# Attention maxima: the causal mask moved from TensorE's matmuls into VectorE's maximum

## The chip, the cores and the metric

One core of a Trainium2 chip runs the whole program in one launch. The metric is the device time in microseconds (us). All data are in float32 unless a line says otherwise; the scores of the attention are made from bf16 parts, three for each number, so that they come out close to float32.

## What is computed

Two hybrid layers act on a residual x of 4 sequences of 1024 tokens with 256 channels: a Mamba block, a feed-forward block, causal attention, the feed-forward block again, then a linear attention, a mixture of experts, a second linear attention with a GELU block, and the mixture of experts again. The change is in the causal attention (16 heads of 16 channels), of which the reference is, cut to what matters:

```python
q, k, v = (split(q), split(k), split(v))
q = apply_rope(q, sin, cos)
k = apply_rope(k, sin, cos)
scores = jnp.einsum('bhqd,bhkd->bhqk', q, k) / jnp.sqrt(jnp.float32(dh))
causal = jnp.triu(jnp.ones((T, T), dtype=bool), k=1)
scores = jnp.where(causal[None, None], jnp.float32(-1000000000.0), scores)
attn = jax.nn.softmax(scores, axis=-1)
out = jnp.einsum('bhqk,bhkd->bhqd', attn, v)
```

## The kernel before

The stages run one after another with a barrier between them. `stage_attn` takes the sequences one by one in a loop of four passes. A pass has two parts: a preparation (norm, projection, rotary embedding, bf16 parts of q and k, their transposes), and `heads(b)`, the attention itself.

In `heads` the 16 heads are taken in four quarters (`QUADS`) of four heads (`HG`, index `j`). The scores are computed twice. First with queries on the partitions (`scores_q`, L1117 to L1128), only for the row maxima: VectorE takes the maximum of every piece in `chunk_max` (L1398). Then with keys on the partitions (`scores_k`, L1130 to L1144), where two extra rows of q and k bring in minus the row's maximum, and ScalarE takes the exponential (`exps`, L1311). `values` (L1156) then multiplies the exponentials by v on TensorE.

A quarter has 12 steps (`PER`), numbered 0 to 11 here. Step by step and for each of its four heads, a piece of `scores_q` has 128, 256, 384, 512, 512, 128, 512, 256, 512, 384, 512 and 512 columns (`CHUNKS`), and a piece of `scores_k` has 512, 384, 256, 128, 512, 512, 512, 512, 512, 384, 256 and 128 (`STEPS`). Of the pieces of `scores_q` those of the steps 0, 1, 2, 3, 5, 7, 9 and 11 end on the diagonal. There a second matmul, identity times the table `causal` (0 and -1e9, bf16), adds the mask onto the last 128 columns (L1126). `scores_k` does the same on its side (L1142); that is not touched.

The order of the work is written out by hand. TensorE runs `scores_q` one whole quarter (`LEAD` = 12 steps) ahead of `scores_k`. So a pass of `heads` begins with 12 steps of `scores_q` alone (called the lead here), goes on with three quarters in which, head by head, `scores_k` and `scores_q` alternate and `values` of the step before closes each step, and ends with one quarter without `scores_q` (the tail). The PSUM banks 0 to 2 are a ring for the pieces of `scores_q`: TensorE waits in `slot` until VectorE has counted `ring_used` for the piece three items back. Banks 3 to 5 are the same for `scores_k`, freed by the exponentials.

Twice a quarter, after step 3 and after step 11, VectorE runs `block_max` (L1410, L1413, L1415: the maximum of a half, its sign turned, and two bf16 parts). TensorE transposes the result in `max_transpose` (L1165) in the following step (step 4 or step 0), behind the `scores_q` of head 1, and waits for it in its order; VectorE copies it out (L1422). In the steps 2 and 6 TensorE also runs `turn` (L1173), whose result VectorE normalises (L1429, L1431).

Of the kernel before, what the change touches and what calls it, by code (L numbers as in the profile page):

```python
# [18 lines left out]
AX = mybir.AxisListType  # L19

P = 128
# [3 lines left out]
GT = 4  # L25
# [941 lines left out]
KS = PARTS * AD  # L967
# [12 lines left out]
SLOTS = 3  # L980
# [4 lines left out]
def stage_attn(c):  # L985
    nc = c.nc
    with Local(c, "attn") as s:
        banks = s.ps("banks", [P, 8, 512])
# [4 lines left out]
        causal = s.sb("causal", [P, 3, P], BF16)  # L993
# [19 lines left out]
        ov = ra[:, :, :, :].rearrange("p a h d -> p (a h d)")  # L1013
        rec = s.sb("rec", [P, 2, GT, HG])
# [5 lines left out]
                 "m_loaded st_filled exp_ready pv_done vh_ready ov_ready rec_ready oT_filled oT_ready y_ready y_used consts zeroed parts_seen")  # L1020
        S = {n: s.sem(n) for n in names.split()}

        def sem(n):
            return S[n]
# [40 lines left out]
        with nc.Block() as block:  # L1065
# [18 lines left out]
            def _(pe):  # L1084
# [32 lines left out]
                def scores_q(b, m, j):  # L1117

                    at_ring = slot(b, ("chunk", m, j))
                    h = m // PER * HG + j  # L1120
                    qt, at, size = CHUNKS[m % PER]
                    diag = at + size == (qt + 1) * P
                    mm = pe.matmul(banks[:, at_ring, 0:size], qT[0:KS, qt // GT, h, qt % GT * P:(qt % GT + 1) * P],  # L1123
                                   kT[0:KS, h, at:at + size], start=True, stop=not diag, skip_group_check=True)
                    if diag:
                        mm = pe.matmul(banks[:, at_ring, size - P:size], causal[:, 2, :], causal[:, 0, :],  # L1126
                                       start=False, stop=True, skip_group_check=True)
                    mm.then_inc(sem("ring_filled"), 1)  # L1128
# [229 lines left out]
            def _(dve):  # L1358
# [39 lines left out]
                def chunk_max(b, m, j):  # L1398

                    qt, at, size = CHUNKS[m % PER]  # L1400
                    item = AT["chunk", m, j]
                    dve.wait_ge(sem("ring_filled"), b * RING + item + 1)
                    dve.tensor_reduce(mp[:, qt // GT, j, qt % GT, at // 512:at // 512 + 1], banks[:, item % SLOTS, 0:size], AX.X,  # L1403
                                      ALU.max).then_inc(sem("ring_used"), 1)
# [51 lines left out]
                dve.memset(mp[:, :, :, :, :], -3e38).then_inc(sem("consts"), 1)  # L1456
                dve.wait_ge(sem("loaded"), 16 * 10)
                dve.wait_ge(sem("lora_filled"), 1)
# [1581 lines left out]
```

## Time and profile before

| | us |
|---|---|
| median of 3 runs | 4031.93 (4028.64 to 4040.47) |
| the profiled execution's own time | 4033.2 |
| its span in the trace | 4031.1 |
| TensorE busy (PE) | 3271.0, 81% of the span |
| VectorE busy (DVE) | 2663.5, 66% |
| ScalarE busy (ACT) | 1691.3, 42% |
| matmul L1123, `scores_q` | 274.3, 768 pieces |
| VectorE L1403, the maxima | 382.2, 768 pieces |

The shares are means over eight different stages. The attention's four passes lie between about 1459 and 2366 us and repeat every 228.6 us; a reader has to look at the windows within one pass. A matmul's busy time is partly the time that its result is under way, so the distance between the starts of two matmuls, not their duration, is what one costs.

### The profile page before, as it was taken

Reading aid. Unit: us, or ns where it says so; the run is one execution under the profiler, and the core shown is the slowest. Engines: PE = TensorE matmul, PEld = TensorE weight load, DVE = VectorE, ACT = ScalarE, POOL = GpSimd, SP = SyncE. Lnnn points to the kernel's source line nnn. Section 1 sums busy time; section 2 is a strip of 40 time slices with the busy share of each in tenths; the row PEclk is TensorE's granted clock in tenths of the full one; section 3 lists DMA queues with packets and bytes.
Section 4 is the critical chain, followed back from the end, with each engine's and each line's share of the span. In section 5 each row is a group of like instructions: output and inputs, shape, how many; then the busy total and the mean of one; then the engine's idle time right before and its main releaser. Section 6 shows DMA issues by size and latency. Waiting matters only on the chain. (4 is left out here: it accounts for less than half of the span.)

```text
span 4031.1 us, 55646 instructions
## 1 busy us (share of the span) xinstructions
PE 3271.0 (81%) x16440; PEld 1865.4 (46%) x16441; DVE 2663.5 (66%) x5097; ACT 1691.3 (42%) x3279; POOL 1379.0 (34%) x1379
## 2 busy tenths in 40 slices
PE   4877787788658969889897989876886788898885
PEld 1333333333225654444444446554465467566464
DVE  2998899899967757575765757597434766223435
ACT  3655545555515535556464655311222223222221
POOL 2777777677730020110202000143454200001453
PEclk9988898899889988979798999988898889999998
DMA  2544545454520000000000000350134578000146
GB/s 89 137 124 118 122 125 126 115 132 129 132 75 1 0 15 2 2 2 2 1 2 2 2 1 0 98 145 0 50 121 138 138 143 96 18 16 0 61 127 199
DMA packets 370275, 283.15 MB, mean 70 GB/s; under 512 B 214026, under 2 KB 290366, under 8 KB 370016
## 3 DMA queue, kind: packets, MB, share of 16 engines
q1 hardware_dynamic: 356960, 246.43, 24.7%
q0 software_dynamic: 13056, 33.65, 2.5%
q8 instruction: 117, 1.92, 0.2%
q14 instruction: 142, 1.16, 0.1%
HBM read 205.69 MB, written 76.16 MB: 70 GB/s over the span
## 5 line engine op out<-in xcount | busy, mean ns | idle before, releaser
L428 POOL TENSOR_TENSOR mamba_dBu<-mamba_du,mamba_bcs 128x512 f32<-128x512 f32 x512 | 642.0, 1269 | 272.1 <-DMA mamba_bcs<-mamba_bc 206.5
L378 PE MATMUL mamba_banks<-mamba_hc,ident 128*128 128x512 f32 x1024 | 557.0, 667 | 214.7 <-DVE mamba_hc L598 152.7
L551 ACT ACTIVATE mamba_banks<-mamba_delta,mamba_a_neg 128x512 f32<-128x512 f32 x512 | 352.1, 691 | 241.2 <-DVE mamba_hc L598 232.2
L1403 DVE TENSOR_REDUCE attn_mp<-attn_banks 128x1 f32<-128x512 f32 (+3 forms) x768 | 382.2, 551 | 96.5 <-PE attn_banks L1126 53.8
L378 PEld LDWEIGHTS mamba_banks<-mamba_hc,ident 128*128 128x128 f32 x1024 | 195.3, 209 | 538.3 <-DVE mamba_hc L598 308.6
L591 DVE TENSOR_TENSOR_SCAN mamba_banks<-mamba_banks,mamba_dBu 128x512 f32<-128x512 f32 x256 | 312.3, 1220 | 92.0 <-POOL mamba_dBu L428 58.0
L598 DVE TENSOR_TENSOR mamba_hc<-mamba_banks,mamba_bcs 128x512 f32<-128x512 f32 x512 | 346.1, 677 | 21.2 <-PE mamba_banks L378 21.1
L591 DVE TENSOR_TENSOR_SCAN mamba_banks<-mamba_banks,mamba_h_end,mamba_dBu 128x512 f32<-128x512 f32 x256 | 329.0, 1286 | 28.7 <-ACT mamba_banks L551 20.6
L1123 PE MATMUL attn_banks<-attn_kT,attn_qT 96*128 96x512 bf16 (+3 forms) x768 | 274.3, 374 | 10.0 <-ACT attn_kT L1292 5.0
L1311 ACT ACTIVATE attn_probs<-attn_banks 128x512 f32<-128x512 f32 (+1 forms) x384 | 182.1, 528 | 180.3 <-PE attn_banks L1142 155.8
L1139 PE MATMUL attn_banks<-attn_qT,attn_kT 98*128 98x512 bf16 (+3 forms) x768 | 248.6, 339 | 10.2 <-ACT attn_probs L1311 5.3
L823 PE MATMUL ffn_hp<-ffn_xT,ffn_w1T 128*128 128x512 f32 x512 | 230.3, 605 | 11.0 <-ACT ffn_xT L160 7.5
L1311 ACT ACTIVATE attn_r<-attn_banks 128x128 f32<-128x128 f32 (+2 forms) x384 | 155.1, 459 | 84.3 <-PE attn_banks L1142 52.6
L1881 POOL DMA_INDIRECT moe_rows<-moe_yb,moe_xg x144 | 141.7, 984 | 137.0 <-issue 73.1
L835 PE MATMUL ffn_yp<-ffn_w2T,ffn_hs 128*128 128x256 bf16 x1536 | 170.0, 273 | 0.0
L835 PEld LDWEIGHTS ffn_yp<-ffn_w2T,ffn_hs 128*128 128x128 bf16 x1536 | 150.3, 98 | 18.4 <-issue 0.7
L823 PEld LDWEIGHTS ffn_hp<-ffn_xT,ffn_w1T 128*128 128x128 f32 x512 | 96.7, 193 | 134.0 <-issue 111.8
L322 PE MATMUL mamba_banks<-mamba_xT,mamba_win 128*128 128x512 f32 x256 | 131.6, 643 | 28.6 <-ACT mamba_sz L504 27.4
L2225 DVE TENSOR_TENSOR moe_h<-moe_hp,moe_silu 128x128 f32<-128x128 f32 x144 | 42.0, 292 | 170.2 <-ACT moe_silu L2070 170.2
L1270 POOL COPY attn_vh<-attn_v 128x512 f32<-128x512 f32 x16 | 13.2, 842 | 408.3 <-PE attn_banks L1156 408.3
L1974 PE MATMUL moe_hp<-moe_we,moe_xgT 128*128 x576 | 152.7, 388 | 0.0
L1139 PEld LDWEIGHTS attn_banks<-attn_qT,attn_kT 98*128 98x128 bf16 x768 | 75.3, 99 | 155.7 <-ACT attn_r L1311 68.7
(374 smaller groups left out, 6584.2 us busy)
## 6 DMA issues: line engine op xcount, KB each, us to landing
mamba_bcs<-mamba_bc SPq DMA_DIRECT2D x256, 512.0 KB, 4.9
moe_slots_moe<-moe_pad SPq DMA_DIRECT2D x2, 9252.0 KB, 52.3
moe_xg<-moe_slots_moe SPq DMA_DIRECT2D x144, 128.5 KB, 2.1
mix_qkv<-mixA_qkv SPq DMA_DIRECT2D x8, 1536.0 KB, 6.0
mixA_y<-moe_rows SPq DMA_DIRECT2D x16, 512.0 KB, 5.7
mix_qk<-mix_qkv SPq DMA_DIRECT2D x16, 512.0 KB, 7.4
mix_v<-mix_qkv SPq DMA_DIRECT2D x16, 256.0 KB, 7.5
mix_out<-mixB_oh SPq DMA_DIRECT2D x16, 256.0 KB, 7.3
```

The lines of the kernel that those rows point to most:

```text
L378: pe.matmul(banks[:, SUMS + k % PAIR, :], c.ident[:, :], hc[:, n % RING, :], start=(st == 0), stop=True, skip_group_check=True).then_inc(s ...
L428: pool.tensor_tensor(dBu[:, n % RING, :], du[:, v, k, :], bcs[:, i_of(n) % 4, 0, :], ALU.mult)\
L551: act.activation(banks[:, n % RING, :], delta[:, v, k, :], ACT.Exp, scale=a_neg[:, k, st:st + 1])\
L591: dve.tensor_tensor_scan(banks[:, n % RING, :], banks[:, n % RING, :], dBu[:, n % RING, :], 0.0 if v == 0 else h_end[:, st, k:k + 1], ALU. ...
L598: dve.tensor_tensor(hc[:, n % RING, :], banks[:, n % RING, :], bcs[:, (p * NS + st) % 4, 1, :], ALU.mult).then_inc(sem("hc_ready"), 1)
L823: mm = pe.matmul(hp[:, b % 4, :], w1T[:, k, b * P:(b + 1) * P], norm.xT[:, k, :], start=(k == 0), stop=(k == KD - 1))
L835: mm = pe.matmul(yp[:, j, :], hs[:, v, b, a, j * P:(j + 1) * P], w2T[:, b, :], start=(b == 0 and a == 0), stop=(b == HB - 1 and a == SP_ - 1))
L1123: mm = pe.matmul(banks[:, at_ring, 0:size], qT[0:KS, qt // GT, h, qt % GT * P:(qt % GT + 1) * P], kT[0:KS, h, at:at + size], start=True, s ...
L1139: mm = pe.matmul(banks[:, bank, 0:size], kT[:, h, kt * P:(kt + 1) * P], qT[:, n % 2, h, at - n % 2 * 512:at - n % 2 * 512 + size], start=T ...
L1311: act.activation(probs[step % 2][:, j, 0:size], banks[:, SLOTS + (step * HG + j) % SLOTS, 0:size], ACT.Exp, scale=AD ** -0.5)\
L1403: dve.tensor_reduce(mp[:, qt // GT, j, qt % GT, at // 512:at // 512 + 1], banks[:, item % SLOTS, 0:size], AX.X, ALU.max).then_inc(sem("rin ...
L1974: mm = pe.matmul(gup[r % 2], xgT[:, r % 2, k * P:(k + 1) * P], we[:, :, :].rearrange("p e n -> p (e n)")[:, bass.ds(at + k * 2 * P, 2 * P) ...
```

## The change

`scores_q` no longer issues the mask matmul; it is one matmul for every piece. A new float32 table `later` of 128 by 512 holds zeros in its first 384 columns and the triangle of the mask in the last 128. In `chunk_max`, a piece that ends on the diagonal is no longer reduced by `tensor_reduce`. VectorE reads the piece from PSUM and the last columns of `later` from SBUF, adds them, writes the sum back to PSUM, and gives the maximum, all by `tensor_tensor_reduce`. In front of it stands a count of a new semaphore, `diag_seen`, which takes the wait for the matmul. The other pieces stay as they are. The table is filled once at the stage's start.

```diff
+        later = s.sb("later", [P, 512])
...
-                    diag = at + size == (qt + 1) * P
-                    mm = pe.matmul(banks[:, at_ring, 0:size], qT[0:KS, qt // GT, h, qt % GT * P:(qt % GT + 1) * P],
-                                   kT[0:KS, h, at:at + size], start=True, stop=not diag, skip_group_check=True)
-                    if diag:
-                        mm = pe.matmul(banks[:, at_ring, size - P:size], causal[:, 2, :], causal[:, 0, :],
-                                       start=False, stop=True, skip_group_check=True)
-                    mm.then_inc(sem("ring_filled"), 1)
+                    pe.matmul(banks[:, at_ring, 0:size], qT[0:KS, qt // GT, h, qt % GT * P:(qt % GT + 1) * P],
+                              kT[0:KS, h, at:at + size], start=True, stop=True).then_inc(sem("ring_filled"), 1)
...
+                    to = mp[:, qt // GT, j, qt % GT, at // 512:at // 512 + 1]
                     dve.wait_ge(sem("ring_filled"), b * RING + item + 1)
-                    dve.tensor_reduce(mp[:, qt // GT, j, qt % GT, at // 512:at // 512 + 1], banks[:, item % SLOTS, 0:size], AX.X,
-                                      ALU.max).then_inc(sem("ring_used"), 1)
+                    if at + size == (qt + 1) * P:
+                        dve.sem_inc(sem("diag_seen"), 1)
+                        dve.tensor_tensor_reduce(banks[:, item % SLOTS, 0:size], banks[:, item % SLOTS, 0:size], later[:, 512 - size:512], 1.0, -3e38,
+                                                 ALU.add, ALU.max, to).then_inc(sem("ring_used"), 1)
+                    else:
+                        dve.tensor_reduce(to, banks[:, item % SLOTS, 0:size], AX.X, ALU.max).then_inc(sem("ring_used"), 1)
...
                 dve.memset(mp[:, :, :, :, :], -3e38).then_inc(sem("consts"), 1)
+                dve.memset(later[:, 0:512 - P], 0.0)
                 dve.wait_ge(sem("loaded"), 16 * 10)
+                dve.tensor_copy(later[:, 512 - P:512], causal32[:, 0, :]).then_inc(sem("causal_at_end"), 1)
+                dve.wait_ge(sem("causal_at_end"), 1)
                 dve.wait_ge(sem("lora_filled"), 1)
```

## Rows read from the trace of the kernel before

**Rows 1.** Windows of pass one: length, busy PE, PEld, DVE, ACT, POOL, PEclk, DMA, GB/s.
```profile
1514.00:1537.40 23.40, 21.14 (x81) 6.88 (x82) 22.40 (x50) 0.00 (x0) 0.00 (x0) 0.57 0.01 1
1537.40:1572.80 35.40, 34.56 (x257) 16.03 (x256) 26.49 (x60) 22.27 (x49) 0.00 (x0) 0.90 0.01 2
1572.80:1606.50 33.70, 32.52 (x270) 15.02 (x266) 26.37 (x61) 22.21 (x50) 0.62 (x1) 1.00 0.01 2
1606.50:1640.20 33.70, 32.52 (x270) 15.02 (x266) 26.36 (x61) 22.21 (x50) 0.61 (x1) 1.00 0.01 2
1640.20:1667.00 26.80, 23.41 (x180) 8.17 (x177) 3.02 (x10) 20.21 (x49) 0.00 (x0) 1.00 0.01 2
```

**Rows 2.** Timeline of VectorE in the lead: start, length, instruction, count, idle before.
```profile
1514.55 6.90 DVE L1403 TENSOR_REDUCE attn_mp<-attn_banks 128x1 f32<-128x128 f32 x16 [3.54 <-PE attn_banks L1126]
...
1523.35 15.37 DVE L1403 TENSOR_REDUCE attn_mp<-attn_banks 128x1 f32<-128x512 f32 x30
```

**Rows 3.** Waits in the lead: who waited for whom, us in total, times, longest.
```profile
PEld attn_banks L1123 <- DVE attn_mp L1403: 14.4, 38, 0.7
```

**Rows 4.** Timeline of TensorE in step 9 of the third quarter, one head and `values`.
```profile
1633.15 0.33 PE L1139 MATMUL attn_banks<-attn_qT,attn_kT 98*128 98x384 bf16 x1
1633.32 0.22 PE L1142 MATMUL attn_banks<-attn_causal 128*128 128x128 bf16 x1
1633.37 0.33 PE L1123 MATMUL attn_banks<-attn_kT,attn_qT 96*128 96x384 bf16 x1
1633.54 0.22 PE L1126 MATMUL attn_banks<-attn_causal 128*128 128x128 bf16 x1
1633.60 0.33 PE L1139 MATMUL attn_banks<-attn_qT,attn_kT 98*128 98x384 bf16 x1
...
1634.58 1.07 PE L1156 MATMUL attn_banks<-attn_probs,attn_vh 128*32 128x512 f32 x8
```

**Rows 5.** Timeline around step 3 and step 4 of the third quarter, VectorE's rows.
```profile
1615.98 2.47 DVE L1403 TENSOR_REDUCE attn_mp<-attn_banks 128x1 f32<-128x512 f32 x4
1618.49 0.19 DVE L1410 TENSOR_REDUCE attn_nm<-attn_mp 128x16 f32<-128x32 f32 x1
...
1620.22 0.20 DVE L1422 COPY attn_nmT<-attn_banks 32x128 bf16<-32x128 bf16 x1
1620.35 1.86 DVE L1403 TENSOR_REDUCE attn_mp<-attn_banks 128x1 f32<-128x512 f32 x4
```

**Rows 6.** The same stretch, TensorE's transpose of the maxima.
```profile
1619.24 0.22 PE L1165 MATMUL attn_banks<-attn_causal,attn_nmb 128*32 128x128 bf16 x1 [0.53 <-DVE attn_nmb L1415]
```

**Rows 7.** Steps 10 and 11 of the third quarter: VectorE's eight maxima, then TensorE's transpose.
```profile
1636.17 4.94 DVE L1403 TENSOR_REDUCE attn_mp<-attn_banks 128x1 f32<-128x512 f32 x8 [0.87 <-PE attn_banks L1123]
...
1641.90 0.22 PE L1165 MATMUL attn_banks<-attn_causal,attn_nmb 128*32 128x128 bf16 x1 [0.85 <-DVE attn_nmb L1415]
```

**Rows 8.** Timeline of TensorE in step 5 of the third quarter, first and fourth head.
```profile
1621.04 0.39 PE L1139 MATMUL attn_banks<-attn_qT,attn_kT 98*128 98x512 bf16 x1
...
1622.20 0.39 PE L1139 MATMUL attn_banks<-attn_qT,attn_kT 98*128 98x512 bf16 x1
```

**Rows 9.** Groups of VectorE's instructions by shape: busy us, mean ns, idle before.
```profile
L598 DVE TENSOR_TENSOR mamba_hc<-mamba_banks,mamba_bcs 128x512 f32<-128x512 f32 x512 | 346.1, 677 | 21.2 <-PE mamba_banks L378 21.1
L591 DVE TENSOR_TENSOR_SCAN mamba_banks<-mamba_banks,mamba_dBu 128x512 f32<-128x512 f32 x256 | 312.3, 1220 | 92.0 <-POOL mamba_dBu L428 58.0 <-ACT mamba_banks L551 32.6 <-issue 0.2
L1403 DVE TENSOR_REDUCE attn_mp<-attn_banks 128x1 f32<-128x512 f32 x384 | 238.7, 682 | 41.3 <-PE attn_banks L1123 38.7 <-PE attn_banks L1126 2.0
```

**Rows 10.** Timeline: four small instructions of VectorE in a row, in the norm.
```profile
1684.44 0.38 DVE L120 BATCH_NORM_AGGREGATE attn_moments<-attn_bn_stats 128x2 f32<-128x6 f32 x4
```

**Rows 11.** Window of the first quarter's start.
```profile
1537.40:1544.50 7.10, 6.79 (x39) 4.15 (x41) 4.44 (x15) 4.28 (x8) 0.00 (x0) 0.50 0.01 1
```

**Rows 12.** Timeline of the stage's start.
```profile
1441.21 0.51 ACT L1334 CAST attn_causal<-attn_ra 128x384 bf16<-128x384 f32 x1 [26.97 <-DMA attn_ra<-in_causal_dram]
...
1445.13 1.42 DVE L1461 SCALAR_TENSOR_TENSOR attn_w<-attn_banks,attn_w 128x256 f32<-128x256 f32 x4 [7.89 <-PE attn_banks L1198]
```

More of the change, by code:

```diff
@@ L1019, in stage_attn @@
                  "stT_filled evac_act evac_dve ring_filled ring_used max_ready part_ready m_ready "
-                 "m_loaded st_filled exp_ready pv_done vh_ready ov_ready rec_ready oT_filled oT_ready y_ready y_used consts zeroed parts_seen")
+                 "m_loaded st_filled exp_ready pv_done vh_ready ov_ready rec_ready oT_filled oT_ready y_ready y_used consts zeroed parts_seen diag_seen causal_at_end")
         S = {n: s.sem(n) for n in names.split()}
```

## The prediction

> **What bounds the kernel now.** The page's chain of work that ended last stays inside the last mixture-of-experts stage and says nothing of the attention. So I read the windows of one pass of `heads` first, and then the timelines of its engines.
>
> The windows [rows 1] show three different parts. In the lead, 23.4 us, VectorE is busy for 22.4 us; TensorE's weight loads for `scores_q` wait 14.4 us for L1403 [rows 3]. The lead is VectorE's. Its 48 maxima, with the first `block_max` between them, run from 1514.55 to 1538.72 us [rows 2], that is 24.2 us. In the second and third quarter, 33.7 us each, TensorE is busy for 32.5 us and VectorE for 26.4 us: these are TensorE's on the whole. The tail, 26.8 us, has no `scores_q` and stays as it is.
>
> Inside a TensorE-bound quarter there are two stretches that VectorE sets nevertheless. After step 3 TensorE reaches the transpose of the maxima and stands for 0.53 us until VectorE's `block_max` is done [rows 6]. VectorE had come to step 3's four pieces at 1615.98 us, right from its normalisation, and went through them without a pause to `block_max` at 1618.49 us [rows 5]. After step 11 the same: eight maxima in a row from 1636.17 us, and then TensorE's stop of 0.85 us [rows 7]. What is added to a maximum there arrives whole at TensorE, and what is taken from TensorE there only makes its stop longer.
>
> **Part 1, the matmuls that go.** A mask matmul costs the distance to the next start, not its 0.22 us: L1126 starts at 1633.54 and the next `scores_k` at 1633.60 us, 0.06 us, and the like one at L1142 takes 0.05 to 0.06 us [rows 4]. I take 0.058 us. 32 of them go per quarter, 1.86 us, but not all of it is gained:
> - Steps 3 and 11: nothing, by the two stretches above.
> - Step 0: the transpose stands behind head 1, so the two matmuls before it only lengthen the stop. Two count.
> - Steps 5 and 7: beside 512-column pieces of `scores_k` TensorE is held by the other ring. In step 5 the fourth head starts 1.16 us after the first [rows 8], though three pairs at (512 + 128 + 128)/2.4 columns per ns make 0.96 us; three matmuls less only lengthen that wait, and the fourth, behind it, counts. In step 7 the pieces are 128 columns longer and the fourth head comes just at 1.16 us, so the limit is reached as soon as something goes. One counts in each.
> - Steps 1, 2 and 9: all four each. In step 9 a head takes TensorE 0.45 us and `values` 1 us more per step, 2.8 us together [rows 4]; VectorE has four pieces shorter than those of 512 columns, under 2.4 us. In the steps 1 and 2 the pieces are no longer.
>
> That is 2 + 8 + 1 + 1 + 4 = 16 matmuls, 0.93 us per quarter, 2.8 us per pass. The first quarter's opening 7.1 us run at a granted clock of 0.50 [rows 11], the 1.2 GHz level, where a matmul costs twice as much: six of the counted ones lie there, 0.3 us more. Together 3.1 us per pass.
>
> **Part 2, the maxima that grow.** The pieces of 512 columns are 0.60 us apart: (2.47 - 0.68) / 3 from the four in a row [rows 5, 9]. An addition with one input in PSUM and one in SBUF takes 677 ns for 512 columns where the maximum takes 682 ns [rows 9], so I cost the adding itself at nothing. The unknown is e, what the second result (the maximum beside the written sum) and the extra count cost. No row of this kernel has an instruction with two results. If the maximum is handed out by a small instruction of its own, the nearest rows are the small ones: four of them in a row end within 0.38 us at 0.16 us each, so 0.07 us apart [rows 10], and the 128-column copy of `block_max`'s result holds the next maximum back by 0.13 us [rows 5], of which half is its columns. That gives e = 0.066 us. If that instruction has to wait until the sum is written out, the distance becomes what `block_max` shows behind the last maximum: it starts at 1618.49 where a plain maximum would have been due at 1615.98 + 4 x 0.60 = 1618.38, and 0.07 us of its own come on top, so 0.11 + 0.07 = 0.18 us. Below, e can be zero if both results leave with one instruction; a gain is excluded, since every column is still read once. I take 0.066 us, and for the 8 pieces of 128 columns in a quarter 0.12 us: the first fifteen pieces of the lead, 307 columns on average, are 0.41 us apart, (6.90 - 0.68) / 15 [rows 2], about 1 ns a column, which leaves some 0.2 us for 128 columns, and there the separate count, its arithmetic and two instructions may no longer hide behind the columns. The mean is 0.08 us.
>
> The Trainium skill bears on both questions. VectorE: DVE Perf Modes, section "Two Vector instructions with no wait between them", says that an operation which also gives out its accumulator is two instructions, the main one and a read of the accumulator. No row here shows it; it would make the case of e = 0 wrong. DVE: opcode table, instruction layouts, handler registers and perf-mode slots says under "Feedback" that a stage reading its own last result loses no cycle, while the scan runs at half rate; the scan's 1220 ns against 677 ns [rows 9] agree with its second half, and by its first the running maximum keeps the full rate.
>
> In the lead all 32 grown maxima lie on VectorE's path: 32 x 0.08 = 2.56 us, less some 0.3 us in the first pieces, where at the 1.2 GHz level TensorE is as slow as VectorE. That is 2.3 us per pass. In the three quarters the four maxima of step 3 and the four of step 11 lie on the path: 8 x 0.066 = 0.53 us, 1.6 us per pass. The other 24 lie beside TensorE's work; their cover is 33.7 - 26.4 = 7.3 us per quarter [rows 1], and they take 1.9 us of it.
>
> **Part 3, waits and the rest.** The count of `diag_seen` waits for the matmul in place of the maximum. Behind it on VectorE stand the piece itself and all later ones; for them TensorE's ring and, after steps 3 and 11, its transpose wait. Where VectorE is behind (the lead, steps 3 and 11) the wait is over before it is reached. Where VectorE waits for TensorE, the start comes some 0.1 us later, and the three banks cover it. The table is filled while VectorE waits anyway: ScalarE gets the mask at 1441.21 us, and VectorE's first work after that is at 1445.13 us [rows 12]. A fill of 384 columns and a copy of 128 are under 1 us. Cost nothing; if that cover were gone, 1 us once.
>
> **The sum.** Per pass + 2.3 + 1.6 - 3.1 = + 0.8 us; four passes, + 3 us. From the profiled execution's 4033.2 us (the span 4031.1 and 2.1 around it) that makes 4036 us. That execution lies 1.3 us above the median, so against the median it is 4035.
>
> **The rivals.** In terms of e, a pass changes by 32 e - 0.3 + 24 e - 3.1 us.
>
> A, the read waits. With e = 0.18 us the lead grows by 5.5 and the quarters by 4.3 us, 6.7 us net per pass: 4033.2 + 27 = 4060 us, slower. It decides from e = 0.12 us on, where the four passes lose 12 us. For it: behind the last maximum `block_max` does start late. Against it: that one waits by a semaphore, and small instructions without one follow closely.
>
> B, one instruction. With e near zero only TensorE's gain is left: 3.1 to 3.4 us per pass, 4033.2 - 13 = 4020 us, at the edge of faster. For it: the busy share of TensorE. Against it: a second result to another memory.
>
> C, half rate. If the running maximum costs a second cycle per column like the scan, a 512-column piece takes 1.2 us, and the mean piece of 320 columns grows by 0.40 us. The lead grows by 12.8 us, and VectorE with 26.4 + 12.8 us becomes the bound of the quarters, 5 us above 33.7: 28 us per pass, 4145 us. Against it: nothing goes back to an earlier point as in the scan.
> The Trainium skill's Vector Engine (DVE) Microarchitecture Reference, section "Points that are easy to get wrong", states a halved rate when both sources of such an instruction lie in SBUF and are not bf16. Here one lies in PSUM; if the rule held all the same, the time would be that of C.
>
> D, the clock. The clock rises to 2.4 GHz some 7 us into the first quarter, after TensorE has been without a long stop [rows 1, 11]. A lead with a less busy TensorE can move that. The first quarter is 1.7 us longer than the others for its 7 us at the low level, so 3.4 us more of it cost 0.8 us per pass, 3 us in all, either way. This widens the range and decides nothing.
>
> That the mask is not removed cannot be: the matmul is gone from the code.
>
> **How the numbers follow.** A difference under 0.3%, 12 us, is about what a measurement of this kernel can't tell from no change. My forecast, e between 0.02 and 0.11 us, 4024 to 4044 us, gets 0.52. A gets 0.26, B 0.14, C 0.04, and 0.04 is for what I have not thought of. Of B about two thirds fall below 4020 us, and of the forecast a little, as my count of gained matmuls may be too small: faster 0.13, slower 0.33, within 0.3% 0.54. The range is to leave out no more than 2 in 10: C, the unknown, and the far ends of A and B, so 4018 to 4064 us.
>
> **What would show it.** In the changed profile: no row of L1126, and yet the second and third quarter shorter by 0.4 us (0.93 less 0.53), not by 1.86 us; the lead grows by 2 to 3 us; the rows of VectorE show the new instruction at about 0.68 us for 512 columns and how far the next piece lies behind it; the stop before the transpose is longer than 0.53 and 0.85 us. A distance of 0.67 us between 512-column pieces would prove e right, 0.78 rival A, 0.60 rival B, 1.2 rival C. The working is wrong if the quarters shorten by over 1 us, which would mean that I was wrong on steps 3, 5, 7 and 11.

## The result and the profile after

| | before | after |
|---|---|---|
| median, us | 4030.91 (4025.62 to 4040.47) | 4040.39 (4032.95 to 4045.51) |
| span of the profiled execution, us | 4031.1 | 4034.1 |
| one pass of `heads`, us | 152.8 | 154.3 |
| preparation between two passes, us | 75.8 | 77.8 |
| attention stage, first matmul to the next stage's first, us | 932.0 | 943.5 |

The ratio is 1.0021, 95% interval 1.0015 to 1.0027: 6 to 11 us more (9.5 by the medians). That is inside the forecast's own range of 4024 to 4044 us and within 0.3%, but three times the 3 us that the sum gave. The two spans are only 3.0 us apart, and that agreement with the sum is chance: in these two executions the attention stage differs by 11.5 us, while stages that nobody touched came out shorter (the linear attention 226.6 and 222.3 us, the two mixture-of-experts stages 291.7 and 288.6, 314.0 and 310.9). So the stage is what must be compared. In this trace its 11.5 us are 5.6 us in the four `heads` and 5.9 us in the three preparations between them.

The first pass of the changed kernel in the windows view answers to [rows 1]: window and length, then busy us (and instructions) of PE, PEld, DVE, ACT and POOL, the granted clock, the DMA share and GB/s. The rows are lead, three quarters, tail and preparation.
```profile
1515.80:1540.70 24.90, 21.96 (x50) 5.16 (x51) 23.97 (x79) 0.00 (x0) 0.00 (x0) 0.50 0.01 1
1540.70:1575.70 35.00, 32.86 (x223) 13.72 (x221) 28.26 (x93) 21.90 (x49) 0.00 (x0) 0.90 0.01 2
1575.70:1609.70 34.00, 31.63 (x239) 13.27 (x236) 28.12 (x93) 21.98 (x50) 0.61 (x1) 1.00 0.01 2
1609.70:1643.30 33.60, 31.33 (x238) 13.24 (x234) 27.99 (x93) 21.88 (x50) 0.61 (x1) 1.00 0.01 2
1643.30:1670.10 26.80, 23.25 (x179) 8.09 (x175) 3.15 (x12) 20.12 (x48) 0.00 (x0) 1.00 0.01 2
1670.10:1748.00 77.90, 59.36 (x407) 44.08 (x407) 44.11 (x116) 37.35 (x52) 26.64 (x38) 0.85 0.01 2
```
The lead grew by 1.5 us. The quarters hold 32 matmuls fewer each, with TensorE busy for 31.3 to 31.6 instead of 32.5 us, and yet are as long as before (35.0, 34.0 and 33.6 against 35.4, 33.7 and 33.7). The last row is the preparation, in which no instruction was changed; the same stretch of the kernel before is this:
```profile
1666.90:1742.70 75.80, 56.72 (x407) 41.81 (x407) 43.40 (x116) 37.28 (x52) 26.55 (x38) 0.89 0.01 2
```
The count of matmuls is the same, and VectorE, ScalarE and GpSimd are busy for nearly the same time. TensorE is busy for 2.6 us longer, and its clock is 0.85 instead of 0.89. The granted clock has two levels here, 0.50 (1.2 GHz) and 1.00 (2.4 GHz), so a mean of c means a share of 2 x (1 - c) at the lower one: 0.22 x 75.8 = 17 us before and 0.30 x 77.9 = 23 us after (17.3 and 23.1 us from the stretches themselves).

The grown maxima, grouped by shape, answer to [rows 9]: busy us, mean ns of one, idle before.
```profile
L1402 DVE CUSTOM_DVE_ANT_0 attn_banks<-attn_banks,attn_later 128x512 f32<-128x512 f32 x128 | 84.6, 724 | 1.8 <-PE attn_banks L1123 1.0
L1402 DVE DVE_READ_ACCUMULATOR2_ANT attn_mp<- 128x1 f32 x512 | 72.2, 141 | 0.6
L1402 DVE CUSTOM_DVE_ANT_0 attn_banks<-attn_banks,attn_later 128x128 f32<-128x128 f32 x128 | 37.7, 301 | 22.8 <-PE attn_banks L1123 19.5 <-PE attn_banks L1161 1.3
L1405 DVE TENSOR_REDUCE attn_mp<-attn_banks 128x1 f32<-128x512 f32 x256 | 160.1, 682 | 26.7 <-PE attn_banks L1123 26.7
```
The one call became two instructions, an addition and a read of the accumulator, which the Trainium skill's section "Two Vector instructions with no wait between them" (VectorE: DVE Perf Modes) said; this trace agrees, 512 of each. What they cost shows in the timeline (start, duration, instruction). After step 3, where [rows 5] had four maxima in 2.51 us:
```profile
1618.98 0.69 DVE L1402 CUSTOM_DVE_ANT_0 attn_banks<-attn_banks,attn_later 128x512 f32<-128x512 f32 x1
1619.59 0.14 DVE L1402 DVE_READ_ACCUMULATOR2_ANT attn_mp<- 128x1 f32 x1
1619.59 0.73 DVE L1402 CUSTOM_DVE_ANT_0 attn_banks<-attn_banks,attn_later 128x512 f32<-128x512 f32 x1
1620.23 0.14 DVE L1402 DVE_READ_ACCUMULATOR2_ANT attn_mp<- 128x1 f32 x1
1620.23 0.73 DVE L1402 CUSTOM_DVE_ANT_0 attn_banks<-attn_banks,attn_later 128x512 f32<-128x512 f32 x1
...
1621.53 0.14 DVE L1402 DVE_READ_ACCUMULATOR2_ANT attn_mp<- 128x1 f32 x1
1621.71 0.19 DVE L1411 TENSOR_REDUCE attn_nm<-attn_mp 128x16 f32<-128x32 f32 x1
```
The read starts together with the next addition, so it is hidden for the most part; only at the end of a run of pieces does it stand alone. The pieces start 0.65 us apart where plain maxima start 0.60 apart: e is 0.05 us, for 512, 384 (0.515 against 0.465) and 256 columns (0.382 against 0.331). For 128 columns, in the first step of the lead, they are 0.31 to 0.34 us apart, against 0.199 for plain maxima that TensorE doesn't hold up, so e is 0.12 us. (In the kernel before those pieces lay 0.214 us apart, because TensorE had two matmuls for each at 1.2 GHz.) The four pieces and the start of `block_max` take 1621.71 - 1618.98 = 2.73 us, 0.22 more than before.

TensorE's stops before the transpose of the maxima, answering to [rows 6] and [rows 7]:
```profile
1622.46 0.21 PE L1161 MATMUL attn_banks<-attn_causal,attn_nmb 128*32 128x128 bf16 x1 [0.74 <-DVE attn_nmb L1416]
...
1645.12 0.22 PE L1161 MATMUL attn_banks<-attn_causal,attn_nmb 128*32 128x128 bf16 x1 [1.06 <-DVE attn_nmb L1416]
```
They were 0.53 and 0.85 us. Both are 0.21 us longer.

### The profile page after: what moved, and what is told of

It reads as the page before. It is cut to its first block and busy times, and to the rows that moved or that the text cites. A ratio compares the mean times of both kernels' runs of the same rounds, so it can differ in the third digit from the quotient of the medians.

```text
span 4034.1 us, 55648 instructions
## 1 busy us (share of the span) xinstructions
PE 3263.4 (81%) x15928; PEld 1843.1 (46%) x15929; DVE 2691.8 (67%) x5611; ACT 1687.1 (42%) x3279; POOL 1383.6 (34%) x1379
## 3 DMA queue, kind: packets, MB, share of 16 engines
q1 hardware_dynamic: 356960, 246.43, 24.7%
## 5 line engine op out<-in xcount | busy, mean ns | idle before, releaser
L378 PE MATMUL mamba_banks<-mamba_hc,ident 128*128 128x512 f32 x1024 | 557.8, 667 | 217.2 <-DVE mamba_hc L598 154.3
L598 DVE TENSOR_TENSOR mamba_hc<-mamba_banks,mamba_bcs 128x512 f32<-128x512 f32 x512 | 344.3, 674 | 19.8 <-PE mamba_banks L378 19.5
L1123 PE MATMUL attn_banks<-attn_kT,attn_qT 96*128 96x512 bf16 (+3 forms) x768 | 278.7, 378 | 19.5 <-DVE attn_mp L1402 6.8
L1402 DVE CUSTOM_DVE_ANT_0 attn_banks<-attn_banks,attn_later 128x384 f32<-128x384 f32 (+3 forms) x512 | 240.5, 517 | 49.8 <-PE attn_banks L1123 43.7
L1885 POOL DMA_INDIRECT moe_rows<-moe_yb,moe_xg x144 | 141.7, 984 | 133.8 <-issue 73.3
L1405 DVE TENSOR_REDUCE attn_mp<-attn_banks 128x1 f32<-128x512 f32 x256 | 160.1, 682 | 26.7 <-PE attn_banks L1123 26.7
```

Of the source, the lines that this page charges most:

```text
L378: pe.matmul(banks[:, SUMS + k % PAIR, :], c.ident[:, :], hc[:, n % RING, :], start=(st == 0), stop=True, skip_group_check=True).then_inc(s ...
L598: dve.tensor_tensor(hc[:, n % RING, :], banks[:, n % RING, :], bcs[:, (p * NS + st) % 4, 1, :], ALU.mult).then_inc(sem("hc_ready"), 1)
L1402: dve.tensor_tensor_reduce(banks[:, item % SLOTS, 0:size], banks[:, item % SLOTS, 0:size], later[:, 512 - size:512], 1.0, -3e38, ALU.add, ...
```

## The experiments

### Gain and cost apart

The first three kernels each do one part of the change. Gain alone: one matmul per piece and the plain maximum, so the maxima are taken of unmasked scores.
```diff
-                    if diag:
-                        mm = pe.matmul(banks[:, at_ring, size - P:size], causal[:, 2, :], causal[:, 0, :],
-                                       start=False, stop=True, skip_group_check=True)
```


> The kernel before without the mask matmuls of scores_q, and with the plain maximum for every piece: part 1 of the sum alone. Left out is the mask for the maxima: a row's maximum takes in the later keys of its diagonal block; the exponentials are masked as before. By my sum only 16 of the 32 matmuls of a quarter are gained: lead unchanged at 23.4 us, second and third quarter 33.7 - 0.93 = 32.8 us, stops before the transpose longer, 3.1 us per pass and 12 us in all, ratio 0.997. If all 32 counted, a quarter would fall by 1.9 us and the ratio would be 0.994. If the repeating pattern of clock stretches settles on another one, a pass can move by 2 us more or less than that, outside heads.

Measured: ratio 0.9980, 95% interval 0.9970 to 0.9989, 7 to 8 us less. `heads` took 148.8 to 150.3 us, 149.7 in the mean. Its second pass in the windows view (lead, first and second quarter of the three that overlap):
```profile
1746.60:1769.50 22.90, 20.72 (x49) 5.08 (x50) 22.23 (x50) 0.00 (x0) 0.00 (x0) 0.50 0.01 1
1769.50:1804.60 35.10, 33.73 (x224) 13.83 (x222) 26.30 (x60) 22.03 (x49) 0.00 (x0) 0.87 0.01 1
1804.60:1837.40 32.80, 31.16 (x238) 13.23 (x234) 26.13 (x61) 21.89 (x50) 0.62 (x1) 1.00 0.01 2
```
The second quarter lost 1.0 us where 0.93 was forecast, and the lead 0.5 us where nothing was. `heads` lost 3.1 us a pass, as forecast, but partly by luck: the first quarter lost 0.8 us in the mean (33.7 to 35.1 us, against 35.3) where 1.2 was forecast. The attention stage fell by less than the four `heads` (8.8 against 12.5 us), because its first preparation, ahead of pass one, took 76.0 instead of 72.9 us in this trace, with 36.3 instead of 31.9 us at 1.2 GHz.

Cost alone: the changed kernel with its mask matmuls kept, so that the mask is added twice.
```diff
+                    if diag:
+                        mm = pe.matmul(banks[:, at_ring, size - P:size], causal[:, 2, :], causal[:, 0, :],
+                                       start=False, stop=True, skip_group_check=True)
```


> The changed kernel with the mask matmuls put back: VectorE adds the table and takes the maximum, TensorE's work is that of before (the mask is added twice): part 2 alone. The changed kernel's trace has the pieces 0.05 us further apart (0.12 us for those of 128 columns). If these simply lie on VectorE's path in the lead and after steps 3 and 11, the lead grows by 32 x 0.067 = 2.1 us, and each quarter by 8 x 0.05 = 0.4 us: 3.4 us per pass, 13.5 us in all, ratio 1.0034. If the clock's pattern takes part, the part of a pass outside heads changes too, by up to 2 us per pass, though no instruction there differs: ratio up to 1.005.

Measured: ratio 1.0049 (1.0036 to 1.0063), 20 us more (22 by the medians). `heads` took 156.7 to 158.2 us, 157.2 in the mean. Its first pass:
```profile
1519.90:1545.20 25.30, 23.27 (x81) 6.20 (x82) 24.19 (x81) 0.00 (x0) 0.00 (x0) 0.53 0.01 1
1545.20:1581.20 36.00, 34.65 (x257) 15.81 (x256) 28.36 (x93) 22.23 (x49) 0.00 (x0) 0.91 0.01 2
1581.20:1615.90 34.70, 32.96 (x271) 14.85 (x268) 28.14 (x93) 22.31 (x50) 0.61 (x1) 1.00 0.01 2
```
The lead grew by 2.0 us (forecast 2.3), each quarter by 0.7 to 0.95 (forecast 0.53). In `heads` the parts add up: against the mean of 152.8 us, 4.4 - 3.1 = + 1.3 us a pass, and the changed kernel has + 1.4 in the mean of its four passes. The cost is larger than forecast in the quarters and smaller in the lead.

Count alone: the kernel before, with only the extra count ahead of each diagonal piece, which takes the wait for the matmul.
```diff
+                    if at + size == (qt + 1) * P:
+                        dve.sem_inc(sem("diag_seen"), 1)
                     dve.tensor_reduce(mp[:, qt // GT, j, qt % GT, at // 512:at // 512 + 1], banks[:, item % SLOTS, 0:size], AX.X,
```


> The kernel before with the extra count of diag_seen ahead of the plain maximum of each piece on the diagonal, and nothing else: the wait is taken by a separate instruction. If the added cost of a piece is the read of the maximum alone, the pieces of 512 columns stay 0.60 us apart and those of 128 columns 0.20 us, and the time is that of before (ratio 1.000). If the separate wait is what makes 128 columns cost 0.12 us more, their distance rises toward 0.3 us, the lead grows by up to 0.8 us, and maxima that wait for TensorE start about 0.13 us later: ratio up to 1.002.

Measured: ratio 1.0030 (1.0019 to 1.0042), 12 us more. That is no less than the whole change costs, and it is not where the count is. The lead took 24.0 instead of 23.4 us, the second quarter 33.9 instead of 33.8. Pieces of 128 columns stay 0.22 to 0.24 us apart in the first step of the lead, so the count by itself does not make the 0.12 us; maxima that wait for TensorE do start 0.11 us later. The sum of the four `heads` even fell, from 611.3 to 608.3 us, because the first quarter of the second, third and fourth pass ran almost wholly at 2.4 GHz. The three preparations rose from 227.5 to 241.3 us. The first quarter of its second pass, and the preparation ahead of that pass:
```profile
1667.00:1747.40 80.40, 61.67 (x407) 45.14 (x408) 44.20 (x116) 37.36 (x52) 26.82 (x38) 0.83 0.01 2
...
1771.30:1804.60 33.30, 32.30 (x257) 14.56 (x255) 26.45 (x60) 21.72 (x49) 0.00 (x0) 0.98 0.01 2
```
The preparation has the same 407 matmuls, but TensorE is busy in it for 61.7 instead of 56.7 us at a clock of 0.83. With an edit of some 0.1 us at some of VectorE's instructions, stretches at 1.2 GHz left the first quarter (1.2 instead of 7.1 us of it) and lay in the preparation (27.3 instead of 17.3 us). One trace shows where they lay; the 12 us of the seven timed runs agree with its stage, 944.0 against 932.0 us.

### A version that masks on the engine that has time

If the step-by-step account is right, the mask belongs to TensorE where VectorE sets the pace (the lead, the steps 3 and 11), and to VectorE everywhere else.
```diff
+        def by_matmul(m):
+            return m < PER or m % PER in (GT - 1, PER - 1)
...
-                    diag = at + size == (qt + 1) * P
+                    diag = at + size == (qt + 1) * P and by_matmul(m)
...
+                    if at + size == (qt + 1) * P and not by_matmul(m):
```


> The changed kernel with the mask matmul and the plain maximum kept in the lead and in the steps 3 and 11, and the added table everywhere else (steps 0, 1, 2, 5, 7 and 9 of the three quarters that overlap with scores_k). If the lead and these two steps are where the longer maxima hurt, nothing is lost any more and TensorE's gain stays: by my sum 0.93 us per quarter, about 3 us per pass, ratio 0.997. If the three banks of the ring do not cover the longer and later maxima, about half of it is left, ratio 0.9985. If the loss lies elsewhere, the ratio is 1.002 as for the whole change.

Measured: ratio 0.9967 (0.9956 to 0.9977), 13 us less than before (16 by the medians), with the full mask. The lead is again 23.4 us, the second and third quarter 33.1 us each, against 33.7 before. `heads` took 150.9, 149.0, 149.9 and 150.9 us. The preparations were unequal among themselves, 76.7, 79.4 and 73.3 us. The last of them:
```profile
2124.20:2197.50 73.30, 53.87 (x407) 40.08 (x408) 43.96 (x116) 37.21 (x52) 26.21 (x38) 0.93 0.01 2
```
Again 407 matmuls, now in 53.9 busy us at a clock of 0.93. The attention stage is 9.0 us shorter than before, 923.0 against 932.0 us. The traced execution as a whole is not (span 4031.0 us, as before; its time lies 17 us above this kernel's median): its Mamba stage took 1151.8 instead of 1147.4 us and other untouched stages were longer too.

### Moving the lead without changing it

The next question was whether a mere shift in time, with no change at TensorE or the maxima, moves the clock. In the kernel before, VectorE fills a scratch tile once, twice or four times before the first maximum of each pass.
```diff
+                    for i in range(4):
+                        dve.memset(pad[:, :], 0.0).then_inc(sem("padded"), 1)
+                        dve.wait_ge(sem("padded"), b * 4 + i + 1)
```


> The kernel before with one fill of an unused tile of 768 columns on VectorE at the start of heads, about 0.8 us, and its wait. Nothing else is changed, neither TensorE's work nor the maxima. If a pass is just the sum of its parts, it grows by 0.8 us and the whole by 3 us, ratio 1.0008. If the repeating pattern of clock stretches matters, a pass can stay at 228.6 us or jump toward 232 us, the difference lying in parts where no instruction changed.

> The same with two fills, 1.6 us, as much as the changed kernel's heads grew by. Plain sum: 1.6 us per pass, 6.5 us in all, ratio 1.0016, and the preparation between two heads as long as before (75.8 us from the last scores_k to the next scores_q). Clock pattern: a pass of 232 us as in the changed kernel, with 77.9 us of preparation, ratio 1.003.

> The same with four fills, 3.2 us. Plain sum: 3.2 us per pass, 13 us in all, ratio 1.0032. Clock pattern: the pass is again 232 us, since it is already that long with half the delay, or jumps once more, to 235 us and more; the preparation then makes up the difference to the sum, in either direction.

Measured, on one chip: 0.9984 (0.9975 to 0.9993), 0.9979 (0.9971 to 0.9988) and 1.0004 (0.9995 to 1.0012). As delays they failed. Four fills, in VectorE's timeline:
```profile
1508.81 0.70 DVE L1439 MEMSET attn_pad<- 128x768 f32 x1 [0.23 <-DVE attn_pad L1439]
1509.64 2.54 DVE L1404 TENSOR_REDUCE attn_mp<-attn_banks 128x1 f32<-128x128 f32 x8
```
VectorE has 3.5 us to wait for TensorE's first piece in any case [rows 2], and four fills only just use that up. The lead stayed at 23.4 to 23.8 us, `heads` at about 153 (but for the first pass of the version with two fills, 150.7 us), the preparations between passes at 75.2 to 76.0, the stage at 931.6, 932.8 and 932.5 us. In that one pass the first quarter had 1.6 us at 1.2 GHz instead of 7, and the preparation ahead of it took 75.9 instead of 72.9 us: a shift like that of the count alone, smaller. The medians differ for all that, by up to 10 us, while in the traces the attention stage is the same to 1.2 us. What differs there lies in the linear attention and the mixture of experts behind it (222.2 and 288.8, 222.1 and 287.7, 226.8 and 291.6 us; before 226.6 and 291.7). The Mamba stage can't be called an effect of the fills: it took 1144.8, 1144.6 and 1142.3 us, and in two traces of the kernel before 1147.4 and 1143.2. So a difference of 0.2% is measurable here and can still say nothing of the edited code. The question itself stays open, since nothing was shifted.

### Both kernels again

> The kernel before once more, unchanged: how far two series of the same program lie apart (ratio 1.000 within 0.001), and whether its profile shows the same clock pattern: 17.3 us at the 1.2 GHz level and 75.8 us of preparation between two heads, 228.6 us per pass. If the pattern differs from execution to execution, one profile of each kernel cannot show what the change did to it.

> The changed kernel once more, unchanged, beside the kernel before on the same chip: ratio 1.002. If its clock pattern belongs to the program, the preparation is 77.8 us again with 23.4 us at the low level. If it is drawn anew each time, the preparation is anything between 73 and 80 us; heads stays at 154.2 us, give or take 1 us for its own low stretch.

Measured: the kernel before against itself 1.0005 (0.9996 to 1.0014), the changed one 1.0023 (1.0013 to 1.0033), as the first time. The stage took 932.7 and 942.1 us. In the changed kernel `heads` again took 154.5 us (153.8 to 155.1), 5.9 us more in the four passes than the kernel before. The preparations between the passes this time were 75.8, 76.8 and 75.7 us, 1.1 more, and the one ahead of the first pass 76.1 against 73.2 us, 2.9 more (in the first pair of traces the two were alike, 73.2 and 72.9). The first of them, changed kernel:
```profile
1672.00:1747.70 75.70, 56.65 (x406) 41.70 (x406) 43.41 (x116) 37.20 (x52) 26.60 (x38) 0.89 0.01 2
```
So the cost in `heads` belongs to the kernel, while the 6 us in the three preparations of the first trace don't come in every execution of it. The unchanged kernel before differs too: 16.5 to 16.6 of the lead's 23.4 us lay at 1.2 GHz in three passes of this trace, 20.0 in all passes of its first trace, and the lead was as long in both.

### Is it the lead's idle TensorE?

One theory was that the lead with fewer matmuls leaves TensorE less busy, and that this keeps the clock low for longer. This kernel is the changed one with the mask matmuls back in the lead alone (where the mask is then added twice).
```diff
-                    diag = at + size == (qt + 1) * P
+                    diag = at + size == (qt + 1) * P and m < PER
```


> The changed kernel with the mask matmuls put back in the lead only, where VectorE is the bound and TensorE has time for them (the mask is added twice there). If the missing activity of TensorE in the lead is what lengthens the low stretch around the start of the first quarter (31.2 us of a heads at the low level against 27.0 us before), it goes back to 27 us and the first quarter loses about 0.5 to 1 us, ratio 1.001. If the low stretch is set by the times at which the parts of a pass fall, nothing changes systematically, and the ratio stays at 1.002.

Measured: ratio 1.0046 (1.0032 to 1.0059), 8 to 9 us above the changed kernel. `heads` is the same, 154.3 to 154.7 us, and 30.7 to 31.6 us of it at the low level did not go back to 27. The preparations took 80.7, 77.8 and 80.5 us, 10.7 us more than the changed kernel had on that chip, which is the whole difference of the stages but 0.5 us (953.3 against 942.1). The first one:
```profile
1674.80:1755.50 80.70, 62.03 (x406) 45.42 (x406) 44.24 (x116) 37.35 (x52) 26.79 (x38) 0.83 0.01 2
```
The theory falls: with more matmuls in the lead the time at 1.2 GHz grew, in this preparation to 27.3 us from 23.1 and 17.3 in the two traces of the changed kernel.

### Gain alone and the selective version again

> The kernel without mask matmuls and without the added table once more (left out is the mask for the maxima alone; the exponentials are masked). Its heads was 150.0 us where the kernel before has 152.8; so four passes give 11 us, ratio 0.9972, if the rest of the program lies as before. It had 0.998 the first time. If it is the better of the two versions, it is not above the selective one here.

> The selective kernel once more. Its heads was 149.0 to 150.9 us, that of the kernel without any mask for the maxima 148.8 to 150.3, so the two should be alike, ratio 0.997 to 0.998; the first time it had 0.9967. Its preparations were 73.3 to 79.4 us with 10.4 to 23.9 us at the low level: if that belongs to the program, a spread of this size comes again, if not, they are 75.8 us.

Measured on another chip, where the kernel before has a median of 4117.14 us: 0.9976 (0.9967 to 0.9986) and 0.9974 (0.9960 to 0.9988). The ratios hold. The 85 us by which everything is longer there lie mostly in the two mixture-of-experts stages (329.6 and 353.9 us in the selective version's trace, 292.4 and 313.2 before); the attention stage took 922.4 and 923.5 us, as on the first chip. Gain alone had `heads` of 149.8, 150.3, 150.0 and 149.7 us and preparations of 77.9, 75.7 and 75.7: as on the first chip, but for the first pass and the preparation behind it (148.8 and 76.8 there). Of the selective version `heads` (151.1, 149.0, 149.9 and 150.9 us) and the preparations (76.7, 79.4 and 73.3 us, with 19.5, 23.9 and 10.3 us at 1.2 GHz) came out as on the first chip to 0.2 us. The pattern of the preparations is thus no accident of one execution of this version. That of the changed kernel did not come again, as shown above.

## Why the prediction was right or wrong, point by point

All kernels in one table, us, lead and second quarter from the first pass, the preparations those between the passes:

| kernel | lead | second quarter | mean `heads` | preparations | stage |
|---|---|---|---|---|---|
| before (two traces) | 23.4, 23.4 | 33.8 | 152.8, 153.0 | 75.8, 76.0, 75.7; 75.8, 75.8, 75.7 | 932.0, 932.7 |
| after (two traces) | 24.9, 24.7 | 34.0 | 154.2, 154.5 | 77.8 each; 75.8, 76.8, 75.7 | 943.5, 942.1 |
| gain alone | 22.8 (others 23.0) | 32.8 | 149.7 | 76.8, 75.8, 75.7 | 923.2 |
| cost alone | 25.3 | 34.7 | 157.2 | 76.1, 75.7, 79.4 | 956.0 |
| count alone | 24.1 (others 23.9) | 33.9 | 152.1 | 80.3, 80.5, 80.5 | 944.0 |
| selective | 23.4 | 33.1 | 150.2 | 76.7, 79.4, 73.3 | 923.0 |
| lead's matmuls kept | 25.3 | 34.0 | 154.6 | 80.7, 77.8, 80.5 | 953.3 |

**Part 1, the matmuls.** The sum was right, 3.1 us a pass, shown by gain alone, and partly by luck. The two quarters at 2.4 GHz gained 0.96 us each for 0.93. The lead's 0.5 us had been left out: at the 1.2 GHz level TensorE sets the pace in its first two steps, where without the mask the maxima follow each other 0.23 to 0.35 us faster in sum, and the first maximum starts 0.1 us sooner. The first quarter gained 0.4 us less than forecast, with about 0.5 us more of it at 1.2 GHz. These two cancel.

**Part 2, the maxima.** e was 0.05 us instead of 0.066 for three of the four sizes and the 0.12 forecast for 128 columns, 0.067 in the mean instead of 0.08. The signs of rival A (0.78 us between pieces), B (0.60) and C (1.2) didn't show: it was 0.65 us. The scan's half rate doesn't apply to a running maximum with one input in PSUM: 724 ns for 512 columns, where the scan takes 1220 [rows 9]. In the lead 32 x 0.067 = 2.1 us; cost alone has 2.0 there, and less the 0.5 of gain alone that is the changed kernel's 1.5.

**Part 3, the waits.** "The three banks cover it" is the step that failed. Step by step in the second quarter (distance between the first `scores_k` of one step and the next, us):

| step | before | gain alone | after | change of after | forecast |
|---|---|---|---|---|---|
| 0 | 2.97 | 2.91 | 3.35 | + 0.38 | + 0.15 |
| 1 | 2.67 | 2.49 | 2.49 | - 0.18 | - 0.23 |
| 2 | 2.95 | 2.72 | 2.92 | - 0.03 | - 0.23 |
| 3 and 4 | 5.89 | 5.89 | 6.12 | + 0.23 | + 0.26 |
| 5 and 7 | 5.24 | 5.11 | 5.11 | - 0.13 | - 0.12 |
| 9 | 2.89 | 2.65 | 2.70 | - 0.19 | - 0.23 |
| 11 | 2.30 | 2.18 | 2.40 | + 0.10 | 0 |

The steps 6, 8 and 10 stayed. The forecast was - 0.40 us; the sum is + 0.2 in this quarter and - 0.1 in the third. Gain alone shows that the matmuls were counted rightly in sum (0.96 for 0.93), though not step by step: step 11 gains 0.12 us where I had nothing, the steps 0 and 1 together 0.1 less than I had. In step 2 it has the whole 0.23 us; with the grown maxima only 0.03 of it is left. Where it goes is in TensorE's and VectorE's rows of the changed kernel, third quarter (first TensorE: the first and the fourth head; then VectorE):
```profile
1615.40 0.33 PE L1123 MATMUL attn_banks<-attn_kT,attn_qT 96*128 96x384 bf16 x1
...
1616.35 0.22 PE L1138 MATMUL attn_banks<-attn_causal 128*128 128x128 bf16 x1
1616.60 0.34 PE L1123 MATMUL attn_banks<-attn_kT,attn_qT 96*128 96x384 bf16 x1
```
```profile
1615.92 0.57 DVE L1402 CUSTOM_DVE_ANT_0 attn_banks<-attn_banks,attn_later 128x384 f32<-128x384 f32 x1 [0.85 <-PE attn_banks L1123]
1616.40 0.14 DVE L1402 DVE_READ_ACCUMULATOR2_ANT attn_mp<- 128x1 f32 x1
```
The first head's row ends at 1615.73 us, but VectorE starts on the piece at 1615.92, 0.19 us later. That is usual here: 0.19 us in the median where VectorE waits for TensorE's piece, 0.15 in the kernel with the count alone, 0.04 in the kernel before. It reads the accumulator until 1616.54. The fourth head needs that bank, and its matmul starts at 1616.60, 0.25 us after the mask of `scores_k` before it, where 0.06 is usual [rows 4]. What VectorE starts later comes back to TensorE through the ring: what three heads save, the fourth gives back. The later start (0.15 us) and e (0.05 us) together are the 0.20 us that step 2 lacks against gain alone. I had counted 24 of the grown maxima as covered by 7.3 us of idle time a quarter; but that idle time lies elsewhere, and three banks are less than the four heads of a step.

In step 11 the count by itself accounts for half of the 0.22 us that lie between gain alone and after: with nothing else changed the step took 2.41 us instead of 2.30. Part 3 took VectorE to be behind there, so that the count would meet no wait. It is not at the step's first piece: counted from the start of step 10's first maximum, in gain alone the matmul ends at 2.36 us and the maximum starts at 2.40; in the changed kernel the same matmul ends at 2.36 us and the addition starts at 2.55.

The excess in step 0 has a second source, in VectorE's timeline at the second quarter's start:
```profile
1577.18 0.18 DVE L1416 TENSOR_TENSOR attn_nmb<-attn_nm,attn_nmb 128x16 bf16<-128x16 f32 x1
1577.78 0.30 DVE L1402 CUSTOM_DVE_ANT_0 attn_banks<-attn_banks,attn_later 128x128 f32<-128x128 f32 x1 [0.42 <-PE attn_banks L1161]
```
From the last instruction of `block_max` to the next piece it is 0.60 us here, from start to start, in the first three passes of both traces; at the third quarter's start 0.25, in the last pass 0.16 at either place, and in the kernel before 0.10 everywhere. Cost alone has the same 0.60 us in three passes, the count alone 0.21 and the selective version 0.25. The piece had been written long before, and the transpose named as the releaser isn't needed for it. The third quarter, without this stop, lost 0.09 instead of 0.38 us in step 0. Why VectorE stands there isn't settled.

The selective version has no grown maxima in steps 3 and 11, and its steps 0 and 3 to 11 gain what gain alone does but for 0.1; its step 2 is 2.92, as after. So its second and third quarters gain 0.65 us, not 0.93. The first quarter gained 0.6 in the two passes where as much of it as before lay at 1.2 GHz (34.7 us, with 7.1 and 7.3 at that level, against 35.3 with 7.1), and 2.6 and 1.4 in the others (32.7 with 1.3, 33.9 with 5.4). So of the 2.7 us that its `heads` gained a pass, 3 x 0.65 = 2.0 are the steps', and the rest came with the clock.

The filling of the table cost nothing, as forecast: VectorE copies it at 1442.54 us and waits 3.7 us more for its next work.

**The sum in `heads`.** Forecast + 0.8 us a pass, measured + 1.5 in the first pass: lead + 1.5 instead of + 2.3, quarters and tail together 0 instead of - 1.5 (- 0.3, + 0.2, - 0.1 and + 0.2, from lengths rounded to 0.1). Two errors partly cancel. Four passes make + 6 us of the measured 6 to 11.

**Rival D, the clock.** "This widens the range and decides nothing" was wrong. I looked for it in the first quarter only and gave it 3 us. It sits in the preparation as much, and there it moved by 14 us in three preparations by the count alone, and by 11 us with the lead's matmuls. Over all kernels the preparation follows its time at 1.2 GHz: 10.3 us give 73.3, 13.3 give 75.2, 17 give 75.7 to 76.8, 19.5 give 76.7 to 76.8, 23 to 24 give 77.8 to 79.4, 27.3 give 80.3 to 80.7, about 0.4 us for each us at the lower level. In the changed kernel it gave 6 us in one trace, and in the other 4: 1 in the three preparations and 3 in the one ahead of the first pass. This is the term that I had mis-sized. With the + 6 of `heads` it makes up, to 0.5 us, the 11.5 and 9.4 us by which the stage differs in the two pairs of traces. How it is spread over the timed runs is not known; their 6 to 11 us leave up to 5 for it.

**What stays open.** What sets the pattern of the clock isn't settled. It is not the pace of TensorE in the lead alone. The preparations came again in two traces of the kernel before and of the selective version, the latter on two chips; gain alone repeated but for one pass, and the changed kernel did not repeat. All other kernels have one trace, so where their low stretches lay is known for one execution each. No run here tells how an edit would move it, and how much of the selective version's 13 us comes from it is only roughly known, from its traces: about 8 us (4 x 2.0) follow from the step table, 3 came with the clock in its first quarters, its preparations are 2 us longer in sum, and the rest is outside the attention stage.

## What to carry to other kernels

Work moved to an engine with idle time is free only if the idle time lies within the ring's reach: count buffers against the pieces of one step, and price the later start, not only the longer instruction. Move it only where the receiving engine isn't the one waited for; here the same edit made `heads` 1.4 us a pass longer where it was made everywhere, and 2.7 us shorter when kept out of the lead and the steps 3 and 11 (2.0 of them by the steps, the rest by the clock in the first quarter). And in a kernel whose TensorE clock changes level, compare the stretches that were not edited too, with their granted clock, before a difference of 0.3% is explained by the edit.

## What the runs showed of the hardware that was not expected

- An addition with a running maximum is an addition and a read of 141 ns that overlaps the next addition; it costs 0.05 us more per piece than a plain maximum, and 0.12 us for 128 columns. The count ahead of it isn't the cause of that: alone it left them 0.22 to 0.24 us apart, not 0.31.
- After a separate count that takes the wait, VectorE starts 0.15 us (plain maximum) to 0.19 us (with the addition) behind the end of TensorE's matmul in the trace, where an instruction with its own wait starts 0.04 us behind.
- At the start of the second quarter VectorE stands for 0.42 us between `block_max` and a piece that is ready, in three passes of four; it is not explained.
- The same 407 matmuls of an untouched stretch took 73.3 to 80.7 us, at granted clocks of 0.93 to 0.83, in kernels that differ only in another part of the pass, one of them by some 0.1 us at single instructions; in two traces of the changed kernel they took 77.8 and 75.8 us.
